# Output projection of batches 0 to 2 moved from the final stage into the attention of batch 7

## What is computed

```
h   = layernorm(x)
q   = h @ Wq.T + bq;  k = ctx @ Wk.T + bk;  v = ctx @ Wv.T + bv     16 heads of 32
p   = softmax(q k^T / sqrt(32) + bias, masked keys at -inf)
x   = x + (p v) @ Wo.T + bo                                         output projection, residual
y   = layernorm(x)
d   = distance of y to each of 32 prototypes
w,i = the two largest of softmax(-d / t), scaled to sum 1
x   = x + sum over the two of w * (A[i] @ (B[i] @ y) + bias[i])     rank 16
```

## Time and profile before

| | us |
|---|---|
| median of 3 runs | 901.77 (899.92 to 902.45) |
| profiled execution | 899.01 |
| its span | 896.8 |
| matmul engine busy (PE) | 848.1 (95%) |
| weight loads busy (PEld) | 751.9 (84%) |
| vector engine busy (DVE) | 610.3 (68%) |
| scalar engine busy (ACT) | 502.0 (56%) |
| GpSimd busy (POOL) | 185.3 (21%) |

### The profile page before, as it was taken

One profiled execution on the slowest core, in us unless ns is written; L12 is line 12 of the kernel. 1 busy time (PEld: TensorE's weight loads), 2 busy tenths in 40 slices (PEclk: granted clock), 3 DMA queues, 4 the chain that ended last, 5 costly groups with the idle time before them and its releaser, 6 DMA issues. The chain is left out here.

```text
span 896.8 us, 20533 instructions
## 1 busy us (share of the span) xinstructions
PE 848.1 (95%) x8016; PEld 751.9 (84%) x8016; DVE 610.3 (68%) x1459; ACT 502.0 (56%) x1066; POOL 185.3 (21%) x240
## 2 busy tenths in 40 slices
PE   6999999999999999999999999999988769999998
PEld 6789898988898889889988989898876647888886
DVE  6586776677666666776686668666678457666664
ACT  5246666665565655666666566666667515444442
POOL 0050112011211201120112011200067233334400
PEclk9999999999999999999999999999999979999999
DMA  8975654675467647565556565546587211222211
GB/s 258 285 161 142 169 148 110 167 173 142 114 165 175 147 110 177 142 143 148 143 134 160 142 155 123 141 108 157 135 200 183 61 51 43 62 62 64 71 30 43
DMA packets 79457, 119.87 MB, mean 134 GB/s; under 512 B 8517, under 2 KB 58797, under 8 KB 79362
## 3 DMA queue, kind: packets, MB, share of 16 engines
q1 hardware_dynamic: 76866, 109.91, 48.8%
q0 software_dynamic: 2496, 8.65, 3.4%
HBM read 79.25 MB, written 39.28 MB: 132 GB/s over the span
## 5 line engine op out<-in xcount | busy, mean ns | idle before, releaser
L566 ACT ACTIVATE score_sb<-score_sb,neg_max 112x750 f32<-112x750 f32 x256 | 236.3, 923 | 74.2 <-DVE neg_max L727 72.4
L727 DVE CUSTOM_DVE_ANT_0 score_sb<-score_ps,neg_bias 112x750 f32<-112x750 f32 x256 | 239.4, 935 | 44.0 <-PE score_ps L906 43.3
L915 PE MATMUL prob_ps<-ident,score_sb 112*125 112x112 f32 x1536 | 248.7, 270 | 8.6 <-ACT score_sb L566 8.0
L915 PEld LDWEIGHTS prob_ps<-ident,score_sb 112*125 112x125 f32 x1536 | 229.9, 188 | 29.7 <-ACT score_sb L566 14.2
L575 ACT ACTIVATE probs_sb<-prob_ps 125x336 f32<-125x336 f32 x256 | 114.7, 448 | 170.5 <-PE prob_ps L915 168.2
L737 DVE COPY probs_sb<-prob_ps 125x336 f32<-125x336 f32 x256 | 129.0, 504 | 117.4 <-PE prob_ps L915 115.2
L902 PE MATMUL score_ps<-k_st,q_st 97*112 97x512 f32 x256 | 105.8, 413 | 0.2 <-DMA q_st<-q_parts 0.2
L475 POOL COPY rsum_wide<-rsum 112x256 f32<-112x256 f32 x32 | 12.7, 398 | 414.9 <-DVE rsum L746 414.9
L861 PE MATMUL acc<-ctx_hi,w_hi 128*128 128x376 f32 (+1 forms) x256 | 88.3, 345 | 7.7 <-DVE ctx_lo L762 7.0
L861 PE MATMUL acc<-ctx_lo,w_hi 128*128 128x376 f32 (+1 forms) x256 | 93.9, 367 | 0.0
L861 PE MATMUL acc<-ctx_hi,w_lo 128*128 128x376 f32 (+1 forms) x256 | 91.1, 356 | 0.0
(11 more groups left out here) (165 smaller groups left out, 1484.4 us busy)
## 6 DMA issues: line engine op xcount, KB each, us to landing
k_st<-k_parts SPq DMA_DIRECT2D x96, 375.0 KB
k_parts<-key_parts SPq DMA_DIRECT2D x60, 188.0 KB, 2.3
k_parts<-key_parts SPq DMA_DIRECT2D x60, 187.0 KB, 5.0
q_st<-q_parts SPq DMA_DIRECT2D x96, 112.0 KB
ctx_raw<-in_ctx_t SPq DMA_DIRECT2D x14, 752.0 KB, 6.7
xb<-in_x SPq DMA_DIRECT2D x8, 448.0 KB, 7.2
attn_t<-attn SPq DMA_DIRECT2D x32, 112.0 KB, 1.9
out<-y_out SPq DMA_DIRECT2D x16, 224.0 KB, 2.3
```

The costliest lines, as they stand in the source:

```text
L566: nc.scalar.activation(scores[:, w % NSC, :], scores[:, w % NSC, :], ACT.Exp, bias=neg_max[:, w % UB:w % UB + 1], scale=-1.0, accum_out=su ...
L727: nc.vector.tensor_tensor_reduce(out=scores[:, w % NSC, :], in0=score_ps[:, at:at + S], in1=neg_bias[:, w // HG % TC, :], scale=1.0, scala ...
L915: last = nc.tensor.transpose(prob_ps[j][0:SW, s * TW:(s + 1) * TW], scores[:, w % NSC, (BT * j + s) * SW:(BT * j + s + 1) * SW], ident[0:T ...
```

## The change

The output projection and the residual of batches 0, 1 and 2 are put into the attention of batch 7, and the final stage projects batches 3 to 7, four ahead of the batch whose distances it is at. What goes with it:

- `project_out` in weave: four matmuls in each of 18 units of batch 7 (`OUT_UNITS`: 8, 10 to 14; 15, 16, 18 to 21; 22 to 24, 26 to 28), two ahead of the second transposes and two behind. They write the two projection accumulators, which are unused in batch 7. The vector engine adds the residual in the unit after each half.
- POOL: the weight chunks start in unit 20 of batch 6 (four of them there) and have two staging buffers, so a chunk's load is issued two chunks ahead; four attended splits and four bias additions (batches 0 to 3) in batch 7, each at a fixed place in its order, each waiting for the users of the buffer it writes.
- SP: the loads of attended values for batches 0 to 3 in units 2, 9, 17 and 24 of batch 7; from the second on, each waits for the split and the bias addition of the batch before.
- Row statistics of batch 0 in units 30 and 31, its root on POOL, the Newton steps and the normalising behind unit 31: the final stage finds y of batch 0 ready.
- The final stage starts with the transposes of y(0) and the projections of 3 and 4. In the loop, batch b + 5 is projected for b = 0 to 2, and nothing for b = 3 to 6. `norm(b + 2)` goes up to just behind the dots, and the scalar engine's order is changed.
- Buffers: at_in and x_res share one buffer with the key and query parts, y2 lies in the context's, x1 of batches 0 to 2 in the first value tensor's.

```diff
-CHUNKS_AT = (4, 6, 7, 9, 10, 12, 14, 15, 17, 18, 20, 22)
+CHUNKS_AT = (20, 23, 26, 29, UB + 1, UB + 2, UB + 3, UB + 9, UB + 10, UB + 13, UB + 17, UB + 18)
+EARLY = 3
+OUT_AT = (8, 15, 22)
+OUT_UNITS = tuple(tuple(u for u in range(first, first + 7) if u % UG != 1)[0:6] for first in OUT_AT)
+SPLITS_AT = {5: 0, 11: 1, 19: 2, 26: 3}
+BIASES_AT = {7: 0, 15: 1, 22: 2, 29: 3}
+ATTENDED_AT = {2: 0, 9: 1, 17: 2, 24: 3}
...
@@ SP, weave @@
-                if b == B - 1 and u == 20:
...
+                if b == B - 1 and u in ATTENDED_AT:
+                    n = ATTENDED_AT[u]
+                    if n == 0:
+                        for r in range(2):
+                            eng.wait_ge(k_stored[r], 32 * (2 + NG * (B - 1)))
+                        eng.wait_ge(q_stored[0], 32 * (1 + 2 * (B - 1)))
+                    else:
+                        eng.wait_ge(sh.at_ready, n)
+                        eng.wait_ge(sh.xb_ready, n)
                     for p in range(2):
...
+                        eng.wait_ge(attn_stored[p], 1 + 32 * (n + 1))
+                    load_attended(eng, sh, x, attn_t, n, sh.at_loaded, sh.xr_loaded)
...
@@ POOL, weave @@
-                if j:
-                    eng.wait_ge(wf_lo_done, i - KT + 1)
-                eng.dma_start(wf_stage[:, k, :], w_dram[j][k * P:(k + 1) * P, :]).then_inc(wf_loaded[k], 16)
+                if i >= 2:
+                    eng.wait_ge(wf_lo_done, i - 1)
+                eng.dma_start(wf_stage[i % 2], w_dram[j][k * P:(k + 1) * P, :]).then_inc(wf_loaded[i % 2], 16)
...
+                if b == B - 2 and u == 12:
+                    eng.wait_ge(ctx_ready[1], KT * B)
+                    for i in range(2):
                         load_weights(i)
...
+                if b == B - 1 and u in SPLITS_AT:
+                    n = SPLITS_AT[u]
+                    if n < 2:
+                        eng.wait_ge(acc_ready, NT * B)
+                    else:
+                        eng.wait_ge(sh.o_ready, TC * (n - 1))
+                    split_attended(eng, sh, at_part[n % 2], sh.at_loaded, n + 1, n, passed)
+                if b == B - 1 and u in BIASES_AT:
+                    n = BIASES_AT[u]
+                    if n == 0:
+                        eng.wait_ge(sh.bo_loaded, 16)
+                        eng.wait_ge(xt_ps_ready, TC * B)
+                    else:
+                        eng.wait_ge(sh.x1_ready, TC * n)
+                    add_output_bias(eng, sh, sh.xr_loaded, n + 1)
+            root(B)
+            widen(B * NG - 1)
...
@@ vector engine, weave @@
+            def residual(b, c):
+                if c == 0:
+                    eng.wait_ge(sh.xb_ready, b + 1)
+                    eng.wait_ge(weigh_done, NG * (B - 1))
+                eng.wait_ge(sh.o_ready, TC * b + c + 1)
+                nc.vector.tensor_tensor(sh.x1_first[:, TC * b + c, :], acc[c][0:TW, :], sh.xb[:, c, :], ALU.add)\
+                    .then_inc(sh.x1_ready, 1)
...
+                for n, units in enumerate(OUT_UNITS):
+                    for c in range(TC):
+                        if w == UNITS - UB + units[3 * c + 2] + 1:
+                            residual(n, c)
+                if w in (UNITS - 2, UNITS - 1):
+                    row_stats(w - UNITS + 2)
+                if w == UNITS - 1:
+                    x_variance(B)
+                if w == UNITS:
+                    newton(B)
+                    normalise_rows()
...
@@ tensor engine, weave @@
+            def project_out(n, m0, m1):
+
+                for m in range(m0, m1):
+                    c, r = divmod(m, 3 * NG)
+                    k, (a, d) = r // 3, PASSES[r % 3]
+                    if m == 0:
+                        eng.wait_ge(sh.at_ready, n + 1)
+                    if r == 0:
+                        if n == 0:
+                            kind, count = tile_count(NT * B - TC + c)
+                            eng.wait_ge(evacuated[kind], count)
+                        else:
+                            eng.wait_ge(sh.x1_ready, TC * (n - 1) + c + 1)
+                    last = nc.tensor.matmul(acc[c][0:TW, :], at_part[n % 2][a][:, k, c * TW:(c + 1) * TW],
+                                            w_part[d][0][:, k, :], start=(r == 0), stop=(r == 3 * NG - 1))
+                    if r == 3 * NG - 1:
+                        last.then_inc(sh.o_ready, 1)
...
+                out = [(n, 4 * units.index(u)) for n, units in enumerate(OUT_UNITS) if b == B - 1 and u in units]
+                for n, step in out:
+                    project_out(n, step, step + 2)
                 if w < UNITS:
                     turn(w, 1)
                 project_steps(b + 1, m[2], m[3])
+                for n, step in out:
+                    project_out(n, step + 2, step + 4)
...
@@ POOL, finish @@
+            def load(b):
+                eng.wait_ge(at_ready, b)
                 eng.wait_ge(xb_ready, b)
                 load_attended(eng, sh, x, attn_t, b, at_more_loaded, xr_more_loaded)
...
+            def split(b):
+                eng.wait_ge(o_ready, TC * b)
+                eng.wait_ge(y2_ready, b - EARLY)
+                split_attended(eng, sh, (at_hi, at_lo), at_more_loaded, b - EARLY, b, passed)
+                eng.wait_ge(x1_ready, TC * b)
+                add_output_bias(eng, sh, xr_more_loaded, b - EARLY)
...
@@ vector engine, finish @@
-            residual(0, 0)
-            residual(0, 1)
-            norm(0)
-            normalise(0)
+            yt_low(0)
+            norm(1)
             small_first()
-            yt_low(0)
+            residual(EARLY, 0)
+            residual(EARLY, 1)
             routing_dot(0)
+            normalise(1)
             small_later()
-            residual(1, 0)
             routing(0)
-            residual(1, 1)
-            norm(1)
             routing_weights(0)
-            normalise(1)
             yt_low(1)
+            residual(EARLY + 1, 0)
+            residual(EARLY + 1, 1)
             for b in range(LAST):
+                ahead = b + EARLY + 2
                 if b:
                     result(b - 1, 1)
                 gate(b)
                 routing_dot(b + 1)
+                if b + 2 < B:
+                    norm(b + 2)
                 gated_low(b)
...
@@ tensor engine, finish @@
+            transpose_y(0)
             for c in range(TC):
-                project_out(0, c, True)
-            transpose_y(0)
+                project_out(EARLY, c)
             eng.wait_ge(pt_ready, 1)
             distances(0)
-            project_out(1, 0)
+            down(0, 0, 0)
             transpose_dot(0)
...
             transpose_y(1)
+            for c in range(TC):
+                project_out(EARLY + 1, c)
             eng.wait_ge(small_ready, 1)
             for b in range(LAST):
+                ahead = b + EARLY + 2
                 transpose_routes(b)
                 distances(b + 1)
-                if b + 2 < B:
-                    project_out(b + 2, 0)
+                if ahead < B:
+                    project_out(ahead, 0)
                     transpose_dot(b + 1)
-                    project_out(b + 2, 1)
+                    project_out(ahead, 1)
                     down(b + 1, 0, 0)
```

More of the change, by code:

```diff
@@ L189, in load_attended, with split_attended, add_output_bias @@
     eng.dma_start(sh.x_res, x[b].rearrange("(c t) e -> t c e", c=TC)).then_inc(xr_loaded, 16)
[L192 removed]
+def split_attended(eng, sh, part, at_loaded, loads, b, passed):
+    hi, lo = part
     eng.wait_ge(at_loaded, 16 * loads)
     apart(eng, passed)
[L196 removed]
+    eng.tensor_scalar(hi[:, :, :], sh.at_in, 1.0, 0.0, ALU.mult, ALU.add).then_inc(sh.at_hi_ready, 1)
     eng.wait_ge(sh.at_hi_ready, b + 1)
[L198 to L199 removed]
+    eng.tensor_tensor(lo[:, :, :], sh.at_in, hi[:, :, :].bitcast(F32), ALU.subtract).then_inc(sh.at_ready, 1)
+def add_output_bias(eng, sh, xr_loaded, loads):
     eng.wait_ge(xr_loaded, 16 * loads)
[L203 removed]
     for c in range(TC):
@@ L229, in weave @@
         ctx_lo = [sb(f"ctx_lo{f}", [P, KT, HC], F32R) for f in range(2)]
+        at_part = [(cut(ctx_hi[0], 0, [P, KT, T]), cut(ctx_lo[0], 0, [P, KT, T])), (sh.at_hi, sh.at_lo)]
         k_st = [sb(f"k_st{p}", [MROW + 1, HG, S], F32R) for p in range(2)]
         q_st = [sb(f"q_st{p}", [MROW + 1, HG, T], F32R) for p in range(2)]
-        v_sb = [sb(f"v_sb{r}", [P, ST, E]) for r in range(2)]
+        v_sb = [sh.v_first, sb("v_second", [P, ST, E])]
         neg_bias = sb("neg_bias", [TW, TC, S])
@@ L322, in weave @@
         attn_ready = sem("attn_ready")
-        wf_loaded = [sem(f"wf_loaded{k}") for k in range(KT)]
+        wf_loaded = [sem(f"wf_loaded{r}") for r in range(2)]
         wf_hi_done = sem("wf_hi_done")
@@ L504, in _ @@
                 split(1, 0, k)
-            for w in range(UNITS + 1):
+            for w in range(UNITS):
                 b, u = divmod(w, UB)
@@ L1010, in finish @@
         at_ready, xb_ready = sh.at_ready, sh.xb_ready
[L1011 to L1012 removed]
```

(19 more changed lines are left out.)

162 lines of the change are left out of this document (73 added, 89 removed).

## The result

| | median us | runs | to the kernel before (95%) |
|---|---|---|---|
| before | 900.89 | 899.92 to 902.45 (4) | |
| after | 884.95 | 883.37 to 889.82 (4) | 0.983 (0.980 to 0.985) |
| forecast | 881.0 | range 873 to 892 | |

What follows compares the result with a forecast made beforehand. Bound: final stage by the tensor engine in its loop and a vector and scalar chain in start-up; batch 7's attention by its score-to-copy ring. 7.1 - 10.8 - 17.1 = -20.8 us from 901.77 gives 881.0 us, range 873 to 892.

Steps and rivals of the forecast that it cites:

- Attention, +7.1: Attention of batch 7: the inserted projection and work around it lengthen it by 7.1 us in all (4 to 20).
- my 0.5 us of stall for the first split: Attention of batch 7, unit 8: first projection matmul waits 0.5 us for attended split 0, 3 us if its load takes 7.9.
- a cycle over 19 us: Sign that the prediction is wrong: a weighing-to-weighing cycle in batch 7's attention over 19 us, where 17.2 was expected.
- 6.3 + 0.3: Attention of batch 7: 18 loaded units grow 0.35 us each, 6.3 us; the last output comes 0.3 us later.
- 18 x 4 x 0.23: Attention of batch 7: the 72 projection matmuls by themselves, given as 16.9 us, the bound if nothing is hidden.
- rival 1: Attention of batch 7: matmuls find no hole and lengthen the softmax turns; attention +17.7, total -10.2, 891.6 us; chance 0.12.
- Loop, -17.1: Final stage, iterations 3 to 5: each loses 5.70 us of projection, 20.26 to 14.56 us, still bound by the tensor engine.
- rival 2: Final stage, short iterations: bound by vector and scalar at 16.5 us each; total -15.0, 886.8 us; chance 0.13.
- Start-up, -10.8: Final stage to the loop's first distances: 25.5 us for 36.3, a gain of 10.8 (8 to 15.4).
- walked 8.3: Start-up: projection of batch 3 done 8.3 us after the first instruction, at a granted clock of 0.66; distances of batch 0 follow.
- I add 1.5 us: Start-up: allowance for vector operations held beside POOL's work, taking the walked 24.0 us to 25.5.
- My upper bound (28.3): Start-up: 28.3 us if three operations meet POOL and are each blocked a full POOL instruction; gain 8.

Runs made afterwards that it cites:

- experiment 1: The changed kernel run again untouched in a later session: 886.61 us, ratio 0.984 to the kernel before.
- experiment 3: Changed kernel with only 12 of the 72 projection matmuls issued in the attention of batch 7, all loads and waits kept (result incomplete): 879.01 us.
- experiment 4: Changed kernel with each of the 72 projection matmuls in the attention of batch 7 issued twice: 900.36 us.
- experiment 7: Changed kernel with the attended load of batch 2 issued one unit later (18 for 17) and its split at unit 20 for 19: 886.04 us.
- experiment 9: Changed kernel with the attended load of batch 2 cut to 16 elements a row of one tile per transfer (that batch's result wrong): 886.84 us.
- experiment 2: Changed kernel with an own semaphore for the prototypes, so widening them no longer waits for all seven small constants: 887.17 us.
- experiment 5: On experiment 2: GpSimd splits 8 of 224 columns and adds bias on 16 of 512 for batches 4 and 5 (results wrong): 883.48 us.
- experiment 6: On experiment 2: root and normalising of batch 1 moved ahead of the six other small constants, nothing left out: 881.39 us, ratio 0.980.
- experiment 10: On experiment 8: two of the four small operations building the bias constants, the copies, moved from vector to scalar: 879.38 us, ratio 0.976.
- experiment 8: On experiment 6: the 72 projection matmuls in batch 7's attention spread over 24 units, three each, instead of 18 with four: 880.36 us, ratio 0.978.

## Why the prediction was short

**Attention, +7.1.** Right in mechanism and in the unit: 1.91 us for 1.93, cycles of 17.13 for 17.2, no wait for a split or for attended values over 1 us. The row statistics and the root at the end hid as walked. The 0.8 us it is over comes from what the walk did not have, the stop of 1.4 to 2.0 us inside a weighing; my 0.5 us of stall for the first split did not come (it was ready at 664.8, its first matmul ran at 666.75). That the sum fits so well is luck in part. From the first weighing to the final stage it is 7.65 us more than before; without what the third cycle has over the second (1.8) it would be 5.8, for a forecast of 6.3 + 0.3 and the stall of 0.5. The stop is also why one of my signs of being wrong, a cycle over 19 us, came close in after (18.96) and came true in experiment 1 (19.51). A single profile places the attention only to some 2 us: in experiment 1 it begins 1.9 us later than in after. Experiments 3 and 4 bear out the central number from both sides. (The prediction's 18 x 4 x 0.23 is 16.6 and not 16.9; its sum does not use it, its rival 1 does.)

**Loop, -17.1.** Right: -16.6, no wait of the tensor engine in the short iterations, so rival 2 is out. Of the two projections' 5.70 us an iteration gives back 5.52 only: in the long iteration they and the 60 matmuls behind them take 2.76 + 2.94 + 8.14 = 13.84 us, in the short one 1.34 + 6.98 = 8.32. The slower start behind the transposed dots falls on whichever matmul comes next.

**Start-up, -10.8.** The step that failed. It came to -5.4 (-7.0 in experiments 1 and 7, -8.5 in 9), and 0.9 us of it went back in iteration 0, where the projection of batch 5 waits for GpSimd's split. Where nobody interferes its steps are nearly as walked: distances of batch 0 at 7.9 us (walked 8.3), the whole 26.05 without GpSimd (24.0). Two things were mis-sized. "I add 1.5 us" for GpSimd beside vector was 4.65 with the constants on time (experiments 2 and 5): three Newton steps and two of the four picks, held until a GpSimd operation ended. My upper bound (28.3) priced three such meetings; there were five, and I had the rule for them. Its words in the prediction, that each lost race costs up to a whole GpSimd operation, are what the runs show: 0.16 us became 1.21, 0.92 became 3.35. And I had the constants in place at once, since today's kernel needs them late. The edit moves their first use from 17.96 us after the stage's first matmul (distances of batch 0 at 732.94 in the trace of before) to 8.3, and the last lands at 8.7. No sentence of the prediction prices that. In the profile of after that delay, with 1.7 us of contention and the half clock behind it, sets the tensor side (the residual of batch 4 waits 1.5 us for it), and vector's side is only 0.4 us later; in experiments 1, 3, 4, 7 and 9 the tensor engine waits for vector there, 0.7 to 5.3 us.

**The sum.** -20.8 was forecast, the medians say -15.9 and the profiled pair -13.2. Of the 7.6 us between forecast and profiled pair, 5.4 are the start-up, 0.9 iteration 0, 0.8 the attention, 0.5 the loop.

## What to carry over

When a step is moved to an earlier place, list what it reads and when each of these lands: a shared semaphore that was harmless behind 15 us of work becomes the bound at the front. Where two chains meet at one point, look at both before mending one; here the first repair brought nothing, and the same with the second on top of it 5 us. And small vector operations that read SBUF alone may not be small beside GpSimd: count each of the kinds named below as held until the GpSimd operation it meets ends, and put them ahead of it (experiment 6), or on scalar (experiment 10).

## What was not expected of the hardware

Beside GpSimd not only operations with two inputs were held. TENSOR_SCALAR on 112 x 2 with one tensor input took 1.22 us for 0.17, CAST of 32 x 512 took 1.78 for 0.40. Others ran at their own length beside the same GpSimd operations: RECIPROCAL on 112 x 2 (0.17 us, experiment 2), TENSOR_SCALAR on 112 x 1 (0.15, experiment 10), and those that read PSUM, as the dot (0.44) and the residual (0.68). The Trainium skill (SBUF — State Buffer, SBUF: two separate sides) covers vector's two-port modes as well as two SBUF inputs; by that rule these agree, if such operations run in those modes, which no view here shows.

The tensor engine stopped for 0.45 to 1.97 us in eight profiles with nothing to wait for that the profile shows. The Trainium skill (Runtime: NRT & Kernel Launch, Instruction fetch mechanics) has blocks of instructions streamed ahead by the engine's sequencer, and the fetch mostly hidden. If the stop is such a fetch, as its order behind the packet suggests, it was not hidden in one dense run of 96 small matmuls and as many weight loads (2.5 us), the third weighing of the last attention.

The granted clock is the other source of spread. In the start-up it fell to half for 10.2 us in after, 6.8 in experiment 1 and 3.4 in experiment 7, with the same 3.5 us of idle beside its fall. In experiments 2 and 5 to 9 it fell for 3.4 to 6.8 us at the start of the last attention too. The tensor engine had been idle for 1.6 us in the 5 us before the first weighing (1.15 and 0.37 us and small pieces), but it was so in all twelve profiles, and in the other six the clock stayed. The first weighing took 3.92 us for 2.51 in experiment 2. Runs of one kernel differ by 6.4 to 7.5 us (experiments 1, 3, 4 and 9). In experiment 3 two runs with a mean granted clock of 0.998 took 875 and 876 us, and two with 0.992 and 0.988 took 882. So the single steps were read from marks inside the profiles.
